# Two transformer layers on one core: another order of the steps, bias rows loaded first, one semaphore for each slot of the two load rings

## The reference, cut to what matters

```python
# layer 0: retention, 8 heads of 32
q, k, v, g = x@w_q+b_q, x@w_k+b_k, x@w_v+b_v, x@w_g+b_g
q, k = theta_shift(q), theta_shift(k)
sim = einsum(q, k / 32**0.5) * decay_mask
r = groupnorm_per_head(sim @ v) * gn_weight + gn_bias
x = layernorm(x + (silu(g) * r) @ w_o + b_o)
# layer 0: feed-forward with weights rounded to -1, 0, 1
x = layernorm(x + (sigmoid(x@Q(w1).T) * (x@Q(w2).T)) @ Q(w3).T)
# layer 1: causal softmax attention, 16 heads of 16
x = layernorm(x + softmax_attention(x) @ Wo + bo)
# layer 1: one shared expert and 8 routed experts, the best 2 for each token
combine = top_2(softmax(x @ W_router.T))
x = layernorm(x + shared(x) * sigmoid(x @ W_sgate.T) + sum_e combine_e * expert_e(x))
```

## Time and profile before

| | us |
|---|---|
| three timed runs | 462.67, 456.79, 460.73 |
| their median | 460.73 |
| the profiled execution | 456.23 |
| its span in the trace | 454.5 |
| PE busy in the span | 367.2 |
| DVE busy | 308.3 |
| ACT busy | 221.6 |
| POOL busy | 176.3 |

### The profile page before, as it was taken

How to read it: one execution, slowest core, us unless ns; L and a number is a source line. 1 busy time by engine, 2 the same in 40 slices (tenths; PEclk the granted TensorE clock), 3 DMA queues, 4 the chain that set the end, 5 groups by cost and what they waited for, 6 DMA issues and landing times.

```text
span 454.5 us, 8254 instructions
## 1 busy us (share of the span) xinstructions
PE 367.2 (81%) x2700; PEld 209.1 (46%) x2700; DVE 308.3 (68%) x807; ACT 221.6 (49%) x460; POOL 176.3 (39%) x216
## 2 busy tenths in 40 slices
PE   0987877889788889888785887787889899998990
PEld 0455645564455533344263443233566545555560
DVE  4666577626577885475479897754888787768635
ACT  4597635344325413787871247655332334545510
POOL 3267576243612002541320013774024452537544
PEclk9989988558979958998989789998999999999996
DMA  7999995001001000043110000114101214153142
GB/s 236 345 259 226 235 235 175 6 35 47 1 3 45 1 1 1 1 136 119 46 48 1 1 1 2 47 53 115 49 24 43 76 61 110 55 164 119 59 129 81
DMA packets 25981, 38.53 MB, mean 85 GB/s; under 512 B 2258, under 2 KB 21266, under 8 KB 25938
## 3 DMA queue, kind: packets, MB, share of 16 engines
q1 hardware_dynamic: 23732, 31.93, 26.3%
q0 software_dynamic: 2208, 6.07, 3.7%
HBM read 30.88 MB, written 17.49 MB: 106 GB/s over the span
## 4 chain that ended last, share of the span: by engine, by line
PE 51%; DVE 23%; ACT 9%; issue 7%; POOL 5%; DMA 3%; SPq 1%; POOLq 0%; DVEq 0%; ACTq 0%
PE psum_a L612 8%; DVE arena_mixers L1332 6%; PE psum_a L890 6%; PE psum_a L749 5%; PE psum_a L904 5%; PE psum_a L859 4%; PE psum_b L612 3%; PE psum_b L821 2%; ACT arena_mixers L1057 2%; DVE cut_weights L1157 2%; PE psum_a L795 1%; POOL arena_mixers L1516 1%; PE psum_b L761 1%; PE psum_a L656 1%; PE psum_b L897 1%
## 5 line engine op out<-in xcount | busy, mean ns | idle before, releaser
L1545 POOL TENSOR_TENSOR ln_rstd<-ln_var_eps,minus_half 128x1 f32<-128x1 f32 x32 | 20.7, 649 | 85.4 <-DVE ln_var_eps L1148 85.3
L612 PE MATMUL psum_a<-cut_weights,x_transposed 128*128 128x512 f16 (+1 forms) x198 | 40.5, 361 | 12.7 <-DVE cut_weights L1157 11.7
L1332 DVE TENSOR_REDUCE arena_mixers<-psum_a 128x2 f16<-128x768 f32 (+3 forms) x44 | 47.3, 1126 | 4.3 <-PE psum_a L795 4.2
L1057 ACT ACTIVATE arena_mixers<-psum_a 128x1024 f32<-128x1024 f32 (+2 forms) x48 | 40.5, 884 | 6.0 <-PE psum_a L811 5.8
L1534 POOL DMA_INDIRECT expert_out<-block_out,arena_ffn x30 | 29.3, 977 | 31.1 <-ACT block_out L1108 25.6
L1562 POOL TENSOR_SCALAR_AFFINE_SELECT arena_mixers<-arena_mixers 128x256 f32<-128x256 f32 (+1 forms) x48 | 24.4, 514 | 40.5 <-ACT arena_mixers L1057 40.2
L890 PE MATMUL psum_a<-cut_weights,stage 128*128 x180 | 32.9, 319 | 7.5 <-issue 3.9
L859 PE MATMUL psum_a<-x_transposed,cut_weights 128*128 128x512 f16 (+1 forms) x144 | 33.0, 380 | 0.7 <-ACT arena_mixers L1057 0.7
L612 PEld LDWEIGHTS psum_a<-cut_weights,x_transposed 128*128 128x128 f16 x198 | 20.2, 107 | 28.3 <-DVE cut_weights L1157 11.7
L1550 POOL TENSOR_TENSOR arena_ffn<-arena_ffn 128x512 f16<-128x512 f32 (+1 forms) x12 | 13.8, 1160 | 48.5 <-ACT arena_ffn L1027 48.5
L1157 DVE SCALAR_TENSOR_TENSOR cut_weights<-stage,cut_weights 128x1024 f16<-128x1024 f32 (+3 forms) x21 | 24.1, 1169 | 7.8 <-ACT cut_weights L925 7.6
(11 more groups left out here) (252 smaller groups left out, 850.4 us busy)
## 6 DMA issues: line engine op xcount, KB each, us to landing
expert_in<-in_row_init SPq DMA_DIRECT2D x1, 10140.0 KB, 53.2
stage<-in_wexp SPq DMA_DIRECT2D x9, 512.0 KB, 3.8
arena_ffn<-expert_in SPq DMA_DIRECT2D x30, 130.0 KB, 2.1
stage<-in_wsh SPq DMA_DIRECT2D x5, 437.0 KB, 10.9
arena_mixers<-expert_out SPq DMA_DIRECT2D x16, 128.0 KB, 2.6
arena_ffn<-in_w SPq DMA_DIRECT2D x1, 1408.0 KB, 7.7
stage<-in_xT SPq DMA_DIRECT2D x2, 512.0 KB, 4.4
stage<-in_wqkvg SPq DMA_DIRECT2D x2, 512.0 KB, 5.3
```

The lines of the kernel that those rows point to most:

```text
L612: ins = mm(dst, lhs[k][a], rhs(k, b, col), start=(k == 0 and a == 0 and b == 0), stop=(bias_at is None and k == n - 1 and a == 1))
L1057: ins = nc.scalar.activation(heads, by_row_tile(ps, se_heads(j))[:, :, :, 0:w], ACT.Exp, scale=1.0 / 16)
L1332: v.tensor_reduce(ST[:, i, 0, h0:h0 + n_h, 48].rearrange("p (h s) -> p s h", s=2), by_row_tile(ps, n_h)[:, :, :, 0:(i + 1) * P], AX.X, ALU ...
```

## The change

ORDER holds the same steps in another order and with other PSUM buffers, and one step more (`cen 0`). The bias rows are the first DMA of the program, two rows of 2049 numbers instead of one row written to two partitions; the last number is the factor that was read from the constants before. Their centring is `cen 0`, ahead of everything; the centring of the two weight pieces is `cen 1` and `cen 2`, each behind the split of the piece before it. For these two pieces ACT first converts the three quarters that are not centred, in two instructions, and then the centred quarter. The staging ring has three semaphores instead of one for each piece. The ring of block rows has one semaphore for each of its ten slots: `bx j` waits for its own block, `bi` for its five, and SP refills a slot as soon as its own block has been transposed.

```diff
--- before.py
+++ after.py
@@ -95,36 +95,38 @@
 ORDER = """
-    split cen cen split split bias split split proj:a0 rot pg:a2 pg:a1 tqk:b1 proj:a2 wsum proj:a1 split split sc:a0
...
+    cen split bias cen split cen split split proj:a1 rot split pg:a0 pg:a2 proj:a1 tqk:b1 wsum proj:a1 split split
...
@@ -139,12 +141,13 @@
...
         return step if condition else None
+    add(("cen", 0))
...
         if i in (1, 2):
-            add(("cen", i), at(i > 1, ("cen", 1)))
-        add(("split", i), at(i, ("split", i - 1)), at(i in (1, 2), ("cen", i)), ("qk", NB - 1, TB - 1) if name == "wexp" and first < EARLY else None)
-    add(("bias", 0), ("cen", 2))
+            add(("cen", i), ("split", i - 1))
+        add(("split", i), at(i, ("split", i - 1)), at(i == 0, ("cen", 0)), at(i in (1, 2), ("cen", i)), ("qk", NB - 1, TB - 1) if name == "wexp" and first < EARLY else None)
+    add(("bias", 0), ("cen", 0))
...
@@ -219,7 +222,7 @@
...
         add(("bx", j), ("sx", b * TB + TB - 1), ("rb", b), ("split", len(PIECES) - 1), at(j >= DEEP, ("bu", j - DEEP)),
-            at(a >= 2 * GROUP, ("bx", a - GROUP - 1)), at(a >= 2 * GROUP, ("bi", a - 2 * GROUP)))
+            at(j >= 2 * GROUP, ("bx", j - 2 * GROUP)), at(a >= 2 * GROUP, ("bi", a - 2 * GROUP)))
...
@@ -359,7 +362,7 @@
         cut = Carve(arena1)
-        bias_raw = cut([8 * D])
+        bias_raw = cut([8 * D + 1])
...
@@ -447,7 +450,7 @@
         pe_done = sem("pe_done")
-        piece_in = [sem(f"piece_in{i}") for i in range(len(PIECES))]
+        piece_in_slot = [sem(f"piece_in_slot{i}") for i in range(NSTAGE)]
...
@@ -479,7 +482,7 @@
...
         sent = [sem(f"tile_sent{t}") for t in range(NT)]
-        blocks_in = [sem(f"blocks_in{a}") for a, _ in GROUPS]
+        block_in_slot = [sem(f"block_in_slot{i}") for i in range(2 * GROUP)]
...
@@ -513,11 +516,11 @@
...
                     sp.wait_ge(rest_cut, NTH[("split", i - NSTAGE)])
-                sp.dma_start(stage[:, i % NSTAGE, 0:n], source[name][:, a:a + n]).then_inc(piece_in[i], 16)
-
+                sp.dma_start(stage[:, i % NSTAGE, 0:n], source[name][:, a:a + n]).then_inc(piece_in_slot[i % NSTAGE], 16)
+
+            sp.dma_start(bias_raw[0:2, :], bias_rows).then_inc(bias_in, 16)
...
             load(1)
-            sp.dma_start(bias_raw[0:2, :], bias_rows.partition_broadcast(2)).then_inc(bias_in, 16)
...
@@ -543,11 +546,12 @@
...
                 if g >= 2:
-                    sp.wait_ge(pe_done, PLACE[("bx", GROUPS[g - 2][1] - 1)][3])
...
                 for j in range(a, e):
+                    if j >= 2 * GROUP:
+                        sp.wait_ge(pe_done, PLACE[("bx", j - 2 * GROUP)][3])
                     row = sp.value_load(blk_r[0:1, j:j + 1], min_val=0, max_val=(NB * SLOTS - 1) * P)
-                    sp.dma_start(XB[:, j % (2 * GROUP), :], expert_in[bass.ds(row, P), :]).then_inc(blocks_in[g], 16)
+                    sp.dma_start(XB[:, j % (2 * GROUP), :], expert_in[bass.ds(row, P), :]).then_inc(block_in_slot[j % (2 * GROUP)], 16)
...
@@ -872,7 +876,7 @@
...
                     j = step[1]
-                    pe.wait_ge(blocks_in[j // GROUP], 16 * GROUP)
+                    pe.wait_ge(block_in_slot[j % (2 * GROUP)], 16 * (j // (2 * GROUP) + 1))
...
@@ -918,14 +922,17 @@
...
                         act.wait_ge(pe_done, PLACE[("qk", NB - 1, TB - 1)][3])
-                    act.wait_ge(piece_in[i], 16)
+                    act.wait_ge(piece_in_slot[i % NSTAGE], 16 * (i // NSTAGE + 1))
+                    dst, src = split_views(i, 0)
                     if i in (1, 2):
-                        act.wait_ge(v_centred, i)
-                    dst, src = split_views(i, 0)
+                        for w in (slice(0, 2 * D), slice(3 * D, 4 * D)):
+                            nc.scalar.activation(dst[:, w], src[:, w], ACT.Copy, scale=SW)
+                        act.wait_ge(v_centred, i + 1)
+                        dst, src = dst[:, 2 * D:3 * D], src[:, 2 * D:3 * D]
...
                     if n == 1:
-                        act.wait_ge(v_centred, 3)
+                        act.wait_ge(v_centred, 1)
...
@@ -1125,6 +1131,13 @@
...
                 dve.wait_ge(pe_done, PLACE[step][3])
+
+            def centre(rows, w, total):
+
+                heads = w.rearrange("p (h d) -> p h d", h=RH)
+                link(v.tensor_reduce(total, heads, AX.X, ALU.add))
+                link(v.tensor_scalar(total, total, -1.0 / RD, None, ALU.mult))
+                v.tensor_tensor(heads, heads, total.unsqueeze(2).to_broadcast([rows, RH, RD]), ALU.add).then_inc(v_centred, 1)
...
@@ -1158,27 +1171,16 @@
...
                     i = step[1]
-                    dve.wait_ge(piece_in[i], 16)
-                    parts = [(P, stage[:, i % NSTAGE, 2 * D:3 * D], v_sum[:, i - 1])]
-                    if i == 2:
+                    if i == 0:
                         dve.wait_ge(bias_in, 16)
-                        parts.append((2, bias_raw[0:2, 2 * D:3 * D], v_sum[0:2, 2]))
-                    for _, w, total in parts:
-                        ins = v.tensor_reduce(total, w.rearrange("p (h d) -> p h d", h=RH), AX.X, ALU.add)
-                    link(ins)
-                    for _, w, total in parts:
-                        ins = v.tensor_scalar(total, total, -1.0 / RD, None, ALU.mult)
-                    link(ins)
-                    for rows, w, total in parts:
-                        heads = w.rearrange("p (h d) -> p h d", h=RH)
-                        v.tensor_tensor(heads, heads, total.unsqueeze(2).to_broadcast([rows, RH, RD]), ALU.add)\
-                            .then_inc(v_centred, 1)
+                        centre(2, bias_raw[0:2, 2 * D:3 * D], v_sum[0:2, 2])
+                    else:
+                        dve.wait_ge(piece_in_slot[i % NSTAGE], 16 * (i // NSTAGE + 1))
+                        centre(P, stage[:, i % NSTAGE, 2 * D:3 * D], v_sum[:, i - 1])
                 elif kind == "bias":
-                    if n == 1:
-                        dve.wait_ge(con_in, 16)
...
                     w = slice(0, 4 * D) if n == 1 else slice(4 * D, 8 * D)
-                    v.scalar_tensor_tensor(bias[0:2, w], bias_raw[0:2, w], con[0:2, C_REST:C_REST + 1], bias[0:2, w],
+                    v.scalar_tensor_tensor(bias[0:2, w], bias_raw[0:2, w], bias_raw[0:2, 8 * D:8 * D + 1], bias[0:2, w],
...
@@ -1424,7 +1426,8 @@
...
                     a, e = GROUPS[g]
-                    dve.wait_ge(blocks_in[g], 16 * (e - a))
+                    for j in range(a, e):
+                        dve.wait_ge(block_in_slot[j % (2 * GROUP)], 16 * (j // (2 * GROUP) + 1))
...
@@ -1624,9 +1627,10 @@
...
     a["w3"] = np.ascontiguousarray(i["L0_ffn_w3"].T)
-    a["bias_rows"] = np.concatenate([i["L0_attn_b_q"][turn], i["L0_attn_b_k"][turn], i["L0_attn_b_v"],
+    row = np.concatenate([i["L0_attn_b_q"][turn], i["L0_attn_b_k"][turn], i["L0_attn_b_v"],
...
                                      i["L1_attn_bv"].reshape(-1), i["L1_attn_bo"]])
+    a["bias_rows"] = np.stack([np.append(row, np.float32(c)) for c in (0.0, SW)]).astype(np.float32)
...
```

60 lines of the change are left out of this document (31 added, 29 removed).

## The result

The changed kernel takes **441.35 us** (median of 439.05, 443.75, 439.91, 442.78), the kernel before 461.28 in the same comparison: ratio 0.9585, 95% interval 0.9495 to 0.9674, faster by 19.9 us. The forecast was 456.5 with a range of 446.5 to 463.5. The profiled execution took 439.05, with a span of 437.2 us where that of before had 454.5. A median here is of all executions, a ratio of those that were not in a slower state of the chip, so the two can differ a little.

A forecast was written before the change was run, and what follows sets the result against it. It took PE as the engine to watch, DVE equally in 234 to 268 us, and priced idle time before PE instructions: 0.3 + 1.4 − 2.0 − 2.5 − 1.0 − 1.4 + 1.0 = −4.2, from 460.73 to 456.5, range 446.5 to 463.5.

The forecast's parts named there:

- rival 2: 75 to 103 us: TensorE's clock stays at the higher level; 451.5 in all, down to 446.5; chance 0.23.
- a: The start: bias rows' cut and centring ahead of the second weight piece delay the first product's second half; +0.3 us.
- b: 25 to 50 us: exchanged PSUM buffers make a projection and the scores wait for ACT; +1.4 us, bounds 0 and +2.7.
- c: 57 to 78 us: three maskings ahead of POOL's layer norm power remove PE's waits of 1.77 and 0.97; -2.0 us.
- POOL's power beside DVE's roundings: 57 to 78 us: power beside one rounding instead of two shortens by an estimated 0.7 us; taken as 0.
- d: 103 to 146 us: moved `dn` products cover PE's gaps, with a new wait before `vr 7`; -2.5 us, bounds 0 and -4.1.
- e: 234 to 268 us: two successive `mx` steps no longer share a buffer, removing a 2.56 wait for DVE; -1.0 us.
- f: First routed block: `bx 0` waits for its own load instead of five, so its 1.37 gap goes; -1.4 us.
- Rival 1: Whole kernel: closed gaps reappear at PE's next wait, so nearly nothing is gained; 460 us, chance 0.24.
- g: Second `bi`, directly behind the first, makes DVE stand for the tenth load; +1.0 us, bounds 0 and +4.3.
- rival 3: Second `bi`: DVE stands the full 4.3 us, again at a later one, and the clock falls once; 463.2, chance 0.13.
- h: The rest: refill per block, staging ring's three semaphores and three ACT conversions change nothing; 0 us.

The follow-up runs named there:

- e10: Kernel before, order unchanged, plus 55 products nobody reads, ahead of PE's waits in retention and in the first batch row's `mx` steps: 448.02 us, ratio 0.972.
- e6: Kernel before with `wo0` of tile 1 and its layer norm's power moved behind the three maskings, in buffer a2: 454.71 us, ratio 0.985.
- e7: Changed kernel with `wo0` of tile 1 moved back ahead of the three maskings: 446.83 us, ratio 0.971 to the kernel before.
- e5: Kernel before plus 36 products nobody reads, ahead of eight PE waits from 63 to 102 us: 450.95 us, ratio 0.979.
- e9: Kernel before with one buffer changed, `mx 1 2 0` writing a2 in place of a0: 460.64 us, ratio 1.000.
- e12: Changed kernel with the second `bi` moved back behind `bu 1`, first run: 439.14 us, ratio 0.953 to the kernel before.
- e14: Changed kernel with the second `bi` behind `bu 1`, run again beside the unedited changed kernel: 438.78 us, ratio 0.954 to the kernel before.
- e1: Changed kernel with the old step order behind the first five pieces; bias rows first, slot semaphores and refill per block kept: 459.87 us, ratio 1.003.
- e11: Changed kernel plus 61 products nobody reads, ahead of its own longest waits: 442.15 us, ratio 0.959 to the kernel before.

## Why the prediction was wrong

The step that failed is the sum itself: it priced every edit as the idle time in front of PE instructions, -4.2 in all, and put the clock at nothing. By e10 the clock is worth 13.2 us and what is left for closed gaps and better order 6.7. The mechanism was in the text, as rival 2 with a chance of 0.23, and too small there: it took the stretch 75 to 103 alone, 10 us less PE time and half of it on the path. The rows give 7.9 less busy time in that piece, and 4.2 to 7.0 us of its length are the clock. The other two places at the lower level, 2.8 and 5.4 us of busy time and 1.7 and 2.5 us of length, I had not priced at all.

The sum's own range is also worked out wrongly. Half of the way from 456.5 to its two ends (449.9 and 469.0) is 453.2 and 462.8, not 452 and 460.5. The measured 441.35 lies below even the favourable end, so no mix of the priced gaps reaches it.

- **a**, +0.3 (0 to +1.3): the first product is done 0.6 later (16.9 against 16.3). Inside the bounds.
- **b**, +1.4: at the end of `proj 5` the changed kernel was 2.2 behind (55.4 against 53.2), in part for the waits for ACT that were meant (0.53 before `proj 2`; the 1.50 before the scores is the old gap), in part at other places (2.64 before `ret 0` at 35.73, 1.66 before `tqk 3`). At the end of `proj 7` it was level again (68.4 against 68.3). Right in kind, worth 0.
- **c**, -2.0: both gaps went. By itself the exchange is worth 4.7 (e6) to 5.5 (e7) in the totals, more than its gaps, since the clock came with it. Mis-sized by a factor of two or more.
- POOL's power beside DVE's roundings, weighed under c: it now takes 1.67 at 60.94 and 2.87 at 66.13, where it was 3.01 and 2.87. The first stands beside one rounding (61.29 to 62.96) and is as short as alone (1.64), so it shortened by all of the difference and not by the half that the estimate of 0.7 had taken. PE did not wait less for it (2.15 in place of 2.00 at `vr 3`). Taking 0 was right.
- **d**, -2.5: the new wait before `vr 7` is 1.02, as predicted (1.0), but the gap before `rx 7` is only cut to 0.61, and the transposes kept 0.47 and 0.79. The stretch is 3.5 shorter. With the old order at the full clock (e5) it is 1.7 shorter, so 1.8 are the order, where 2.5 was forecast: right in kind, a little too large.
- **e**, -1.0 (0 to -2.6): 2.9 less, of which 1.5 idle. The reason given, the shared buffer, is refuted by e9.
- **f**, -1.4: the gap is gone, and 0.58 and 0.76 stand before the next two blocks. Rival 1's mechanism, a wait that reappears one step further on. Worth about 0.
- **g**, +1.0 (0 to +4.3): DVE stood 4.24, to a tenth what the rows said; the cost is some 3 by the stretches, 1 to 3 by the totals (e12, e14). I should have taken the price of rival 3, since nothing stood between the two `bi`.
- **h**, 0: e1 shows it.
- **Rival 1** is right of single gaps (e9, f). That PE's idle time changed by only 1.1 us over the whole kernel does not speak for it: at a faster clock the same order has PE wait longer (5.45 for 4.80 in e5's second stretch), so an unchanged idle time already means that gaps were closed.

What stays open: which property of the two orders' waits lets the clock fall in the one and not in the other, beyond that filling the waits of the old order stops it; which moves other than c's hold it in retention; why the same order falls to the lower level for a longer time in some executions than in others (e14's 32.0 against 29.3); and which moves give the 6.7 us that are not the clock.

## What to carry to other kernels

Where a profile shows a long stretch at the lower clock level with PE busy most of it, price it first, and then ask which waits stand at its start. Of what PE's busy time lost here, about half or more came off the length by the clock (4.2 to 7.0 of 7.9, 1.7 of 2.8, 2.5 of 5.4). A change of order is not the sum of the gaps it closes. PE's busy time for the same work, before and after, tells that the clock moved; it does not tell how much of the gain is the clock. For that the old order has to be seen at the same clock, as the filled kernels show it. A wait for a later load is cheap on an engine only behind the work that others wait for: check what is queued behind it.

## What the runs showed that was not expected

Work that nobody reads made the kernel faster: 36 products, 8 to 10 us less; 55 products, 13 us less. It did so in an order in which PE stood again and again, and did nothing in the order that already held the clock (61 products: 442.15 against 441.35). A fall that is prevented at one place can appear at another that was free of it (e10 at 116 us, e11 at 111 and 148 us), so the gain of a place is not the gain of the kernel.
